# Attention stage of a graph network: marks folded into the reciprocal, pairs of output and square tiles added on VectorE, half the norm matmuls, messages weighed one group ahead

## The reference, cut to what matters

```
alpha = e / (s[dst] + 1e-16)                  # s: sum of e over the edges of a destination
msg = h[src] * alpha[:, :, None]
out = jax.ops.segment_sum(msg, dst, num_segments=n).reshape(n, H * C)
out = out + gat_bias
mean = jnp.mean(out, axis=0)
var = jnp.var(out, axis=0)
```

## Time and profile before

| | |
|---|---|
| median of 3 runs | 2927.1 us (2925.19 to 2933.04) |
| the profiled execution | 2935.7 us, its span 2934.2 us |
| attention stage in the trace | 1612 to 1858 us after the start of the span |
| one group of the stage in its steady part | 4.66 us |
| busy in the whole span | PE 75%, DVE 62%, ACT 62%, POOL 49% |

### The profile page before, as it was taken

How to read it: one execution, slowest core, us unless ns; L and a number is a source line. 1 busy time by engine, 2 the same in 40 slices (tenths; PEclk the granted TensorE clock), 3 DMA queues, 4 the chain that set the end, 5 groups by cost and what they waited for, 6 DMA issues and landing times. The chain is left out here.

```text
span 2934.2 us, 52033 instructions
## 1 busy us (share of the span) xinstructions
PE 2190.3 (75%) x11215; PEld 1489.9 (51%) x11215; DVE 1814.1 (62%) x8347; ACT 1823.1 (62%) x4630; POOL 1440.1 (49%) x1442
## 2 busy tenths in 40 slices
PE   3376666666664777758885899666663999999996
PEld 1154444444443666648885444333332566666663
DVE  8787676766764666648886555466664544445552
ACT  0097777777774888859994333599995344444442
POOL 5177777777774666537771000000001366666663
PEclk9888888888886999988997999798997999999998
DMA  1155555555453555546662665499998111222210
GB/s 41 35 177 159 171 159 162 168 155 175 153 160 96 150 160 158 155 133 181 198 199 61 179 169 163 132 320 311 315 311 245 46 49 55 57 59 59 60 53 24
DMA packets 488297, 426.56 MB, mean 145 GB/s; under 512 B 54823, under 2 KB 384702, under 8 KB 488138
## 3 DMA queue, kind: packets, MB, share of 16 engines
q1 hardware_dynamic: 423946, 350.44, 39.7%
q0 software_dynamic: 64192, 74.09, 9.9%
HBM read 234.05 MB, written 194.13 MB: 146 GB/s over the span
## 5 line engine op out<-in xcount | busy, mean ns | idle before, releaser
L1982 POOL DMA_INDIRECT x_bx<-t_X,k_bslot x2 | 2.0, 1016 | 670.4 <-DMA t_X<-x_ve 670.1
L2235 POOL DMA_INDIRECT out_dram<-mlp_ou,mlp_iro x200 | 200.0, 1000 | 186.4 <-issue 185.8
L461 POOL DMA_INDIRECT second_xs<-t_X,second_irs x200 | 212.5, 1063 | 133.4 <-ACT second_m L1151 56.4
L461 POOL DMA_INDIRECT first_rd<-t_R,a_irs x200 | 203.4, 1017 | 119.0 <-issue 60.3
L2228 POOL DMA_INDIRECT mlp_xs<-t_X,mlp_irs x200 | 202.2, 1011 | 78.3 <-issue 59.7
L461 POOL DMA_INDIRECT a_xd<-in_x_dram,a_ird x200 | 207.9, 1040 | 65.7 <-issue 60.3
L461 POOL DMA_INDIRECT a_xs<-in_x_dram,a_irs x200 | 203.7, 1018 | 60.8 <-issue 60.5
L461 POOL DMA_INDIRECT project_xs<-t_X,project_irs x200 | 200.7, 1004 | 65.7 <-issue 62.2
L2278 DVE TENSOR_TENSOR mlp_v<-mlp_ps_r,mlp_b 126x512 f32<-126x512 f32 x50 | 34.6, 692 | 278.9 <-ACT mlp_y L2336 275.6
L2379 PE MATMUL mlp_ps_e<-mlp_h,mlp_we 128*128 128x504 f32 x400 | 188.4, 595 | 1.2 <-ACT mlp_h L2358 1.2
L2139 PE MATMUL x_ps_o<-x_ht,x_wd 128*128 128x512 f32 (+1 forms) x198 | 128.9, 738 | 80.7 <-ACT x_ht L2090 80.7
(11 more groups left out here) (391 smaller groups left out, 7036.4 us busy)
## 6 DMA issues: line engine op xcount, KB each, us to landing
t_X<-first_x SPq DMA_DIRECT2D x194, 256.0 KB, 3.1
first_x<-in_x_dram SPq DMA_DIRECT2D x97, 256.0 KB
project_x<-t_X SPq DMA_DIRECT2D x97, 256.0 KB, 3.1
x_x<-t_X SPq DMA_DIRECT2D x97, 256.0 KB, 6.3
t_X<-x_x SPq DMA_DIRECT2D x97, 256.0 KB, 6.0
out_dram<-x_ou SPq DMA_DIRECT2D x97, 256.0 KB, 6.7
t_G<-second_g SPq DMA_DIRECT2D x50, 267.8 KB
t_X<-first_xo SPq DMA_DIRECT2D x50, 252.0 KB
```

Source lines behind the costliest of these rows:

```text
L461: pool.indirect_dma_start(dst[:, q, :], None, table, bass.IndirectOffsetOnAxis(ap=idx[:, q:q + 1], axis=0)).then_inc(s_rows, 16)
L2235: pool.indirect_dma_start(out, bass.IndirectOffsetOnAxis(ap=iro[s][:, q:q + 1], axis=0), OU[s][:, q, :], None, bounds_check=N - 1, oob_is_ ...
```

## The change

The marks `lastc` are multiplied into the reciprocal (a new instruction of 126 x 16 on VectorE), so that `o` is zero in every row that isn't the last of its destination. Then the norm sums need no marks: VectorE adds blocks 0 and 1 of `o` with its squares to blocks 2 and 3 (new, 126 x 512, into `sm`), and TensorE multiplies only the two sums by a column of ones. Own of group t stands in two halves behind the S of blocks 1 and 3 of group t-1, where it stood before its own group's first S; the norm matmuls stand behind the S of blocks 0 and 2. VectorE weighs group t+1 behind the `o` of group t-2, and `m` and `u` have four buffers instead of two. Squares are unchanged.

```diff
@@ -1697,11 +1697,12 @@
     sb, sem = m.sb, m.sem
     Ge = [sb(f"ge{i}", [RW, GT, 128]) for i in range(4)]
     Gd = [sb(f"gd{i}", [RW, GT, 128]) for i in range(4)]
-    M = [sb(f"m{i}", [RW, GT, MW]) for i in range(2)]
-    U = [sb(f"u{i}", [RW, GT, MW]) for i in range(2)]
+    M = [sb(f"m{i}", [RW, GT, MW]) for i in range(4)]
+    U = [sb(f"u{i}", [RW, GT, MW]) for i in range(4)]
     den = sb("den", [RW, GT, H])
     rec = sb("rec", [RW, GT, H])
     OS = [sb(f"o{i}", [RW, GT, 2, 128]) for i in range(4)]
+    SM = [sb(f"sm{i}", [RW, 2, 256]) for i in range(2)]
     row = sb("row", [1, 256])
     psO = [m.ps(f"o{i}", [128, 1024]) for i in range(2)]
     psN = m.ps("norm", [128, 512])
@@ -1711,6 +1712,7 @@
     s_m, s_u, s_ci, s_co = sem("messages"), sem("own"), sem("carry_in"), sem("carry_out")
     s_de, s_re, s_fr, s_o, s_sq, s_n, s_bn = (sem("denominator"), sem("guarded"), sem("reciprocal"), sem("out"), sem("squares"),
                                               sem("norm_sums"), sem("sums_out"))
+    s_mk, s_ad = sem("masked"), sem("added")
     s_nr, s_nc = sem("norm_row"), sem("norm_columns")
     s_os = m.ring("out_stored", 4)
     block = m.ctx.enter_context(nc.Block())
@@ -1751,19 +1753,22 @@
 
     @block.vector
     def _(dve):
-        def body(t, u):
-            r = u % 2
-            if there(t, NGE):
-                cols = bass.ds(t * GT, GT)
-                dve.wait_ge(s_ge[u], landed(t, u, 4))
-                dve.wait_ge(s_gd[u], landed(t, u, 4))
-                if not before(t, 2):
-                    dve.wait_ge(s_co, (t - 1) * GT)
-                for dst, src, p, done in ((M[r], Ge[u], sx.P, s_m), (U[r], Gd[u], sx.PS, s_u)):
+        def weigh(g, s):
+            if there(g, NGE):
+                cols = bass.ds(g * GT, GT)
+                dve.wait_ge(s_ge[s], landed(g, s, 4))
+                dve.wait_ge(s_gd[s], landed(g, s, 4))
+                if not before(g, 4):
+                    dve.wait_ge(s_co, (g - 3) * GT)
+                for dst, src, p, done in ((M[s], Ge[s], sx.P, s_m), (U[s], Gd[s], sx.PS, s_u)):
                     dve.tensor_tensor(dst[:, :, 0:128].rearrange("p q (h c) -> p q h c", h=H),
                                       src[:, :, :].rearrange("p q (h c) -> p q h c", h=H),
                                       p[:, cols, :].unsqueeze(3).to_broadcast([RW, GT, H, C]), ALU.mult)
                     dve.tensor_copy(dst[:, :, 128:MW], p[:, cols, :]).then_inc(done, 1)
+
+        weigh(0, 0)
+
+        def body(t, u):
             g, s = t - 2, (u - 2) % 4
             rg = s % 2
             if there(g, NGE):
@@ -1774,17 +1779,28 @@
                 dve.tensor_scalar(den[:, :, :].rearrange("p (b q) h -> p b q h", b=2), num[:, :, :, 128:MW], 1e-16, None, ALU.add).then_inc(s_de, 1)
                 dve.wait_ge(s_de, g + 1)
                 dve.reciprocal(rec[:, :, :], den[:, :, :]).then_inc(s_fr, 1)
+                dve.wait_ge(s_fr, g + 1)
+                dve.tensor_tensor(rec[:, :, :], rec[:, :, :],
+                                  kp.lastc[:, bass.ds(g * GT, GT)].unsqueeze(2).to_broadcast([RW, GT, H]), ALU.mult).then_inc(s_mk, 1)
                 if not before(g, 4):
                     dve.wait_ge(s_os[s], landed(g - 4, s, 4))
-                    dve.wait_ge(s_n, g - 3)
-                dve.wait_ge(s_fr, g + 1)
+                    dve.wait_ge(s_ad, g - 3)
+                dve.wait_ge(s_mk, g + 1)
                 for b in range(2):
                     ins = dve.tensor_tensor(OS[s][:, 2 * b:2 * b + 2, 0, :].rearrange("p q (h c) -> p q h c", h=H),
                                             num[:, b, :, 0:128].rearrange("p q (h c) -> p q h c", h=H),
                                             rec[:, 2 * b:2 * b + 2, :].unsqueeze(3).to_broadcast([RW, 2, H, C]), ALU.mult)
                 ins.then_inc(s_o, 1)
-
-        steps(dve, NGE, 3, 3, body)
+            weigh(t + 1, (u + 1) % 4)
+            g, s = t - 4, u
+            if there(g, NGE):
+                dve.wait_ge(s_sq, g + 1)
+                if not before(g, 2):
+                    dve.wait_ge(s_n, g - 1)
+                dve.tensor_tensor(SM[s % 2][:, :, :], OS[s][:, 0:2, :, :].rearrange("p q w d -> p q (w d)"),
+                                  OS[s][:, 2:4, :, :].rearrange("p q w d -> p q (w d)"), ALU.add).then_inc(s_ad, 1)
+
+        steps(dve, NGE, 5, 3, body)
         dve.wait_ge(s_n, NGE)
         dve.tensor_copy(row[:, :], psN[0:1, 0:256]).then_inc(s_nr, 1)
         dve.wait_ge(s_nc, 1)
@@ -1792,64 +1808,67 @@
 
     @block.scalar
     def _(act):
-        def carry(g, r, q):
+        def carry(g, s, q):
             if not there(g, NGE):
                 return
+            r = s % 2
             if q == 0:
                 act.wait_ge(s_m, g + 1)
             if before(g, 1) and q == 0:
-                act.activation(M[r][0:1, q, :], kp.zrow[0:1, 0:MW], ACT.Copy).then_inc(s_ci, 1)
+                act.activation(M[s][0:1, q, :], kp.zrow[0:1, 0:MW], ACT.Copy).then_inc(s_ci, 1)
                 return
             act.wait_ge(s_co, g * GT + q)
             rp, o = (r, column(q - 1)) if q else (1 - r, column(GT - 1))
-            act.activation(M[r][0:1, q, :], psO[rp][0:1, o:o + MW], ACT.Copy).then_inc(s_ci, 1)
-
-        def body(t, u):
-            g1, r1 = t - 1, (u - 1) % 2
-            carry(g1, r1, 0)
-            carry(g1, r1, 1)
+            act.activation(M[s][0:1, q, :], psO[rp][0:1, o:o + MW], ACT.Copy).then_inc(s_ci, 1)
+
+        def body(t, u):
+            g1, s1 = t - 1, (u - 1) % 4
+            carry(g1, s1, 0)
+            carry(g1, s1, 1)
             g, s = t - 3, (u - 3) % 4
             if there(g, NGE):
                 act.wait_ge(s_o, g + 1)
                 act.activation(OS[s][:, :, 1, :], OS[s][:, :, 0, :], ACT.Square).then_inc(s_sq, 1)
-            carry(g1, r1, 2)
-            carry(g1, r1, 3)
+            carry(g1, s1, 2)
+            carry(g1, s1, 3)
 
         steps(act, NGE, 4, 2, body)
 
     @block.tensor
     def _(pe):
-        def norms(g, s, qs):
+        def norms(g, s, b):
             if not there(g, NGE):
                 return
-            if qs[0] == 0:
-                pe.wait_ge(s_sq, g + 1)
-            for q in qs:
-                k = g * GT + q
-                ins = pe.matmul(psN[0:1, 0:256], kp.lastc[:, k:k + 1], OS[s][:, q, :, :].rearrange("p w d -> p (w d)"),
-                                start=k == 0, stop=k == NT - 1)
-            if qs[-1] == GT - 1:
+            if b == 0:
+                pe.wait_ge(s_ad, g + 1)
+            ins = pe.matmul(psN[0:1, 0:256], kp.ones[0:RW, 0:1], SM[s % 2][:, b, :], start=g == 0 and b == 0, stop=g == NGE - 1 and b == 1)
+            if b == 1:
                 ins.then_inc(s_n, 1)
 
-        def body(t, u):
-            g, r = t - 1, (u - 1) % 2
-            gn, sn = t - 4, u
-            if there(g, NGE):
-                pe.wait_ge(s_u, g + 1)
-                if not before(g, 2):
-                    pe.wait_ge(s_o, g - 1)
-                for b in range(2):
-                    pe.matmul(psO[r][0:RW, 512 * b:512 * b + 2 * MW], kp.ident[0:RW, 0:RW],
-                              U[r][:, 2 * b:2 * b + 2, :].rearrange("p q w -> p (q w)"), start=True, stop=False, skip_group_check=True)
+        def own(g, s, b):
+            if there(g, NGE):
+                if b == 0:
+                    pe.wait_ge(s_u, g + 1)
+                    if not before(g, 2):
+                        pe.wait_ge(s_o, g - 1)
+                pe.matmul(psO[s % 2][0:RW, 512 * b:512 * b + 2 * MW], kp.ident[0:RW, 0:RW],
+                          U[s][:, 2 * b:2 * b + 2, :].rearrange("p q w -> p (q w)"), start=True, stop=False, skip_group_check=True)
+
+        def body(t, u):
+            g, s = t - 1, (u - 1) % 4
+            gn, sn = t - 5, (u - 5) % 4
             for q in range(GT):
                 if there(g, NGE):
                     gate(kp, pe, s_ci, g * GT + q + 1)
                     o = column(q)
-                    pe.matmul(psO[r][0:RW, o:o + MW], kp.S0[:, bass.ds(g * GT + q, 1), :].rearrange("p a e -> p (a e)"),
-                              M[r][:, q, :], start=False, stop=True, skip_group_check=True).then_inc(s_co, 1)
-                norms(gn, sn, (q,))
-
-        straight(NGE, 5, body)
+                    pe.matmul(psO[s % 2][0:RW, o:o + MW], kp.S0[:, bass.ds(g * GT + q, 1), :].rearrange("p a e -> p (a e)"),
+                              M[s][:, q, :], start=False, stop=True, skip_group_check=True).then_inc(s_co, 1)
+                if q % 2 == 0:
+                    norms(gn, sn, q // 2)
+                else:
+                    own(t, u, q // 2)
+
+        straight(NGE, 6, body)
         pe.wait_ge(s_nr, 1)
         pe.matmul(psC[:, 0:1], row[:, 0:128], kp.ones[0:1, 0:1], start=True, stop=True)
         pe.matmul(psC[:, 1:2], row[:, 128:256], kp.ones[0:1, 0:1], start=True, stop=True).then_inc(s_nc, 1)
```

## The result

The changed kernel has a median of 2896.75 us (2894.88 to 2901.23, 4 runs) beside 2929.18 us (2925.19 to 2933.04, 4 runs) before: ratio 0.9892, 95% interval 0.9873 to 0.9911. The forecast was 2895 in 2883 to 2909. A ratio compares fast executions alone, those within 1.5% of their kernel's fastest. The profiled execution is the slowest of the four, 2901.2 us with a span of 2899.5 for 2934.2.

The account below looks back on a forecast made before the run. Bound: attention's ring of S, carry, next S, plus own, which isn't hidden. 45 turns from 4.66 to 3.99 us (30.2), head 1.4 and tail 0.5 save 32.1 of 2927.1: 2895 us, range 2883 to 2909.

Parts of the forecast that it names:

- The ring and the slots: S, its carry, next S: 0.94 us a block with a norm matmul, 0.91 with half an own; four make 3.70.
- The new wait: Own's first half waits for `o`, ending 1.70 us behind the carry (1.57 to 1.82); this makes the period 3.99 us.
- VectorE's cover: VectorE's work from `den` on takes 3.51 us of the 3.99 us period, leaving 0.48 us a group.
- The attribution: Claimed that the unhidden 1.83 us of a group hold one block and all of own, whose halves go into gaps.
- Steady term: 45 turns, fifth group to last but one, each going from 4.66 to 3.99 us: 30.2 us saved.
- Head: First four turns of the attention stage: 1.4 us saved, of which 0.7 in the first (bounds 0 and 1.9).
- Tail: From the last S to the copied row, 6.23 us before: 0.5 us saved, bounds -0.5 and 1.5.
- The sum: Steady turns, head and tail of the attention stage together: 32.1 us saved, from 2927.1 to 2895 us.
- Weights not pulled ahead: Own's weights don't load while S streams: period 4.19 us, 2904 us in all; chance 0.10.
- The tile early enough: `o` ends before own needs it, so own doesn't wait: period 3.70 us, 2882 us in all; chance 0.05.
- The clock: TensorE streams less and its granted clock falls to half: 6.0 us a group, 2987 us if all cold; chance 0.03.
- signs of being wrong: `den` waits for nothing, a norm matmul waits for a sum of pairs, or `o` ends outside 1.57 to 1.82 us.

Follow-up runs that it names:

- last-two-S version: Changed kernel with norm matmuls behind S of blocks 0 and 1, halves of own behind blocks 2 and 3: turn 3.72 us, ratio 0.9888.
- no-marks run: Changed kernel with the marks left out of the reciprocal: turn 3.73 us, ratio 0.9866.
- doubled sum of pairs: Changed kernel with the sum of pairs made twice, once into a spare tile: turn 4.11 us.
- the run with two: Changed kernel with the marks multiplied in twice: turn 4.20 us, 4.16 without one turn at the slow clock.

## Why the prediction was right, step by step

- **The ring and the slots.** Right to 0.01 us: 0.94 with a norm matmul, 0.91 with half an own whose weights are pulled ahead (changed kernel and the last-two-S version).
- **The new wait.** Right in place and size: own's load stands 0.44 later than right behind S (1725.33 for 1724.56 + 0.33), 0.4 was forecast, and 0.29 of it lengthens the turn. That the output tile ends 1.71 us behind the carry (1.70) is luck in its terms, two errors that cancel: `den` starts 0.03 behind the carry's end and not 0.10, and the marks cost 0.35 and not 0.28. The 0.10 was read from the earlier trace rows, which stands behind the loop; the changed kernel's last groups have 0.11 there too (1803.91 to 1804.02). The no-marks run shows that this wait is all that lies between 3.99 and the ring's 3.71.
- **VectorE's cover.** 3.51 and 0.48 us were right, by the doubled sum of pairs and by own behind the last two S. The rows of the changed kernel itself give 3.56 (1723.54 to 1726.49, and 0.61). The 0.38 that the row of `den` shows understates the cover by 0.07 to 0.1, since an instruction could begin 0.61 behind the start of the sum, 0.07 ahead of its end.
- **The attribution failed.** "The two halves of own are what the change puts into gaps" reads the gain into own's new place. The runs show the opposite: with own bare and ahead of its group the turn is 3.92, and with own in the slots but four norm matmuls it is 4.67. What was not hidden before was the norm matmul behind the last S: its 0.52 us, the 0.09 ahead of it and the 0.11 of own's bare weights behind it are the 0.72 by which the last slot shrinks with own bare (1.72 to 1.00), where own runs beside the carry. The sum came out since it added slots, whatever was named as the cause. The slot of 1.72 before, with its own load at 1725.63:

```profile
1724.69 0.29 PEld L1848 LDWEIGHTS attend_ps_o<-attend_m,k_S 126*126 126x126 f32 x2 [0.44 <-issue]
...
1726.41 0.41 PEld L1848 LDWEIGHTS attend_ps_o<-attend_m,k_S 126*126 126x126 f32 x2
```

- **Steady term.** 45 x (4.66 - 4.00) = 29.7 for 30.2. In the last groups, outside the loop, turns are 4.02 to 4.05 (one 4.39).
- **Head.** Mis-sized: 1.4 forecast, 0.5 measured. Three turns took 14.33 us (1613.64 to 1627.97) for 14.06, where 0.8 less was expected, and the fourth 3.89 for 4.66, as expected. The clock was granted in full only from about 1624, some 10 us behind the first S, where it had been 7 before. The two other executions of the changed kernel took 18.28 and 17.59 us for the four turns, 0.5 and 1.1 less than before, so this term scatters from one execution to the next:

```profile
1620.00:1624.00 4.00, 3.29 (x10) 2.47 (x10) 1.79 (x6) 0.93 (x4) 0.00 (x0) 0.50 0.62 166
1624.00:1630.00 6.00, 4.20 (x20) 2.80 (x19) 4.66 (x16) 2.65 (x8) 0.00 (x0) 1.00 0.57 154
```

- **Tail.** 5.69 us (1814.88 to 1820.57) for 6.23: 0.5, as forecast.
- **The sum.** The stage saved 30.8 us for 32.1. The medians saved 32.4; that they come nearer to the forecast than the stage does is luck, since the other phases scatter by more than that. The prediction's own range of 2889 to 2902 takes head and tail at their bounds by its words, but its lower end adds 1.9, the values taken; with the bounds (head 2.7, tail 1.5) it would be 2887.
- **Rivals.** Weights not pulled ahead: out, by the load at 1726.94, 0.22 behind S's. VectorE the bound: out, with 0.45 to 0.48 to spare. The tile early enough: out, 10.3 us of wait. The clock: the grant is 1.00 through the steady part, though TensorE streams less. Of the signs of being wrong none came: `den` waits 0.41, and no wait of a norm matmul for a sum of pairs is in the answer.

## What to carry to other kernels

Where a ring across engines sets the pace, work off the ring is free as long as each slot holds no more than the ring's own length, so count what stands in each slot, not what an engine does in sum: a norm matmul worth 0.52 us showed 0.03 in three slots, and in the fourth its removal gave 0.72. When work is moved earlier, look for the buffer that it now asks for: here one slot earlier or later for own's first half decided 0.28 us a group. A row's share of a path is its busy time plus its hand-over: 0.17 us of marks were 0.35. And read a hand-over where the work will stand: a row from behind the loop was 0.07 off inside it.

## What the runs showed of the hardware

- Behind S, the one-column weights of norm load 0.42 us after S's own and own's 126-column weights 0.22, so weights are not pulled ahead across this change. By the prediction's count of passes it costs 0.09 us each way, an estimate from column counts. With own between S and norm it is the same (0.65 from own's load at 2060.10 to norm's, of which 0.11 is the rest of S and 0.44 own).
- A small VectorE instruction with an address row ahead of it, behind a wait, begins 0.14 to 0.17 us behind the end of the one that it depends on (the marks in the loop, 2020.45 to 2020.59 and 1724.00 to 1724.17); without one it is 0.04 (`den` to reciprocal, 1723.71 to 1723.75, and the marks in the last groups, 1804.48 to 1804.52). That the address row is the reason is argued, not shown: the second marks instruction of the run with two begins 0.03 behind the first one's end.
- Chips differ by 11 to 15% on the kernel before (medians of 3258, 3272 and 3360 us for 2929), and the changed kernel's times go with it. From the traces of the changed kernel on the first chip and the last, nearly all of it (374 of 412 us) stands ahead of the attention stage, in the phases that gather rows. The phase named `first` on the first chip, changed kernel:

```profile
140.00:900.00 760.00, 509.29 (x2431) 358.22 (x2432) 540.70 (x2596) 582.61 (x1466) 576.17 (x563) 0.86 0.53 162
```

and on the last one, the same kernel:

```profile
153.00:1130.00 977.00, 565.77 (x2476) 397.67 (x2476) 577.64 (x2610) 599.80 (x1488) 580.09 (x561) 0.75 0.43 127
```

The windows are close to the whole phase, which takes some 988 us for 780. GpSimd is busy for about as long (576 and 580 us), TensorE for 11% longer at a granted clock of 0.75 for 0.86, and the transfers run at 127 GB/s for 162. Which of these is the cause, and what makes it so on that chip, was not tried.
